# Loading the first layer's weights from a clear queue, and starting fc1 on three of four batches

## The chip, the cores and the metric

One core of a Trainium2 chip runs the kernel. The metric is the device time of one execution in microseconds; lower is better. Before the change the median of three runs is 1658.18 us (1657.36 to 1660.54).

## The reference

`x` is 64 batches of 128 rows by 512, all in float32. Two residual layers follow each other:

```
x = x + (einsum('bsd,bdh->bsh', x, W[cat_ids]) + b[cat_ids])          # layer 0
h = gelu(einsum('bnd,hd->bnh', x, fc1_w) + fc1_b)                      # 512 -> 2048
x = x + concat([einsum('bnh,sh->bns', h, fc2_w) + fc2_b,               # 2048 -> 384
                einsum('bnh,bph->bnp', h, experts_w[idx]) + experts_b[idx]])   # 2048 -> 128
```

`cat_ids` picks one of 64 matrices W of 512x512 for every batch, `idx` one of 16 expert matrices of 128x2048.

## The kernel before

The 64 batches go in 16 groups of four (GB = 4). Each float32 operand is split into a high part, rounded to fp32r by ScalarE, and a low part, which VectorE makes as the difference; every product is three fp32r matmuls (high by high and the two mixed ones). An operand x, y or weight is turned first where the contraction wants it, as four 128x128 transposes on TensorE (line 745) or by VectorE.

**The prologue** (before the first `groups` body) does layer 0 of the first four batches. A batch has four slices of its W (`KD` = 4), 256 KB each; slice j is `l0_slice(0, j)`. SyncE loads the slices (`load_w`, lines 340 to 349), eight slots deep; four of the slots lie in `w_raw`, four in `e_blocks`. Its order is written by hand in lines 399 to 420: the table `cats`, x of batch 0, a wait for `cats`, then the slices with, between them, one row of the bias b0 for each batch, the next batch's x, the table `exps`, fc1's bias `b1`, a wait for `exps` and four reads of that table; then the experts' weights. ScalarE casts a slice (`w_high`), VectorE subtracts (`w_low`), TensorE multiplies (line 784) and adds the bias row by a matmul of one row (line 782). `y_sum` adds x to the result on VectorE, `turn_y` transposes it on TensorE, `y_high` and `y_low` split it into `y_t`.

fc1 and fc2's own weights come through `load_prep(t)` on ScalarE's queue, are transposed by `turn_prep(t)` and split by `prep_high(t)` and `prep_low(t)`: tiles 0 to 4 beside the prologue, from tile 5 on two in each step of the first group. From tile 5 on, `turn_prep(t)` waits until `prep_low(t - 1)` is done, since all use the bank `ps_t`.

**The groups' loop** has 16 chunks c of 128 hidden columns. TensorE's `fc1(g, c)` is 12 matmuls of 512 columns (four batches of 128 rows side by side), into `ps_e` for even and `ps_h` for odd c; ScalarE applies `gelu`, VectorE splits the result into `h`; `fc2(g, c)` is 12 matmuls of 512 columns. Two slices of the next group's layer 0 stand between them in some chunks. All queues run in the order that the program writes; semaphores hold them together. In the first chunk the program before writes, for ScalarE, `gelu(0, 0)` and then `prep_high(5)` and `prep_high(6)`; for VectorE `h_high`, `prep_low(5)`, `h_low`, the turn of the next experts, `prep_low(6)`.

## Time and profile before

| | us |
|---|---|
| median of the runs | 1658.18 |
| the profiled execution's own time | 1657.96 |
| its span | 1656.2 |
| TensorE busy | 1637.2 |
| VectorE busy | 1314.8 |
| ScalarE busy | 554.1 |
| DMA moved | 243.44 MB |

The profile is of one execution. Its span, from the first to the last instruction, lies 1.8 us under that execution's own time. TensorE is busy for 99% of the span; a busy time counts an instruction that runs at half the clock with its full length. The page's slices are 41 us long, so that the prologue, which ends near 40 us, fills the first; questions about it go to the views by time.

### The profile page before, as it was taken

The numbers are of one execution on the slowest core, as the hardware profiler recorded it, in microseconds if no ns is written. First come the engines' busy times: TensorE is split into PE (matmuls) and PEld (weight loads), VectorE is DVE, ScalarE is ACT, GpSimd is POOL, SyncE is SP. The second block draws the span as 40 slices with busy tenths as digits, with TensorE's granted clock in tenths as the row PEclk, the third lists the DMA queues.
The fourth block names the chain that finished last, engine by engine and source line by source line (L and its number), as shares of the span: only waits on it lengthen the run. The fifth ranks groups of instructions, "written<-read, shape, count | busy, mean of one in ns | idle before, by whom it ended". The sixth has DMA issues, their size and how long they took to land.

```text
span 1656.2 us, 27997 instructions
## 1 busy us (share of the span) xinstructions
PE 1637.2 (99%) x7064; PEld 1320.6 (80%) x7064; DVE 1314.8 (79%) x2004; ACT 554.1 (33%) x926; POOL 214.4 (13%) x195
## 2 busy tenths in 40 slices
PE   7999999999999999999999999999999999999999
PEld 4788887888888888888888888888888887888887
DVE  5787978788787887877878788787878878788865
ACT  4343333333333333333333333333333333333321
POOL 0110200202020120200202011020200202002100
PEclk8899999999999999999999999999999999999999
DMA  7665555546465454664546555454654546555410
GB/s 218 175 187 136 164 151 155 144 139 167 130 175 145 143 157 115 174 161 142 153 115 183 146 161 142 141 159 133 168 157 135 152 114 180 162 144 148 134 52 26
DMA packets 303178, 243.44 MB, mean 147 GB/s; under 512 B 34152, under 2 KB 234984, under 8 KB 303084
## 3 DMA queue, kind: packets, MB, share of 16 engines
q1 hardware_dynamic: 255852, 203.75, 45.1%
q10 hardware_dynamic: 47232, 38.82, 7.7%
q14 instruction: 82, 0.67, 0.1%
q8 instruction: 12, 0.20, 0.1%
HBM read 209.93 MB, written 32.51 MB: 146 GB/s over the span
## 4 chain that ended last, share of the span: by engine, by line
PE 97%; issue 1%; SPq 1%; DMA 1%; DVE 1%; ACT 0%; DVEq 0%
PE ps_out L812 42%; PE ps_e L797 21%; PE ps_h L797 21%; PE ps_y L784 10%; PE ps_t L745 1%; PE ps_h L784 0%; SPq L316 0%; DMA x_blocks<-in_x 0%; DMA e_blocks<-in_L_cond_W 0%; DMA exps<-in_itok_B 0%; SPq L348 0%; PE ps_e L745 0%; PE ps_h L782 0%; DVE w_split L602 0%; DVE y L637 0%
## 5 line engine op out<-in xcount | busy, mean ns | idle before, releaser
L812 PE MATMUL ps_out<-w2e,h 128*128 128x512 f32 x3072 | 756.6, 395 | 0.0
L812 PEld LDWEIGHTS ps_out<-w2e,h 128*128 128x128 f32 x3072 | 575.5, 188 | 137.8
L797 PE MATMUL ps_e<-y_t,w 128*128 128x512 f32 x1536 | 378.2, 396 | 0.5 <-DVE y_t L602 0.5
L797 PE MATMUL ps_h<-y_t,w 128*128 128x512 f32 x1536 | 376.4, 394 | 0.0
L797 PEld LDWEIGHTS ps_e<-y_t,w 128*128 128x128 f32 x1536 | 289.1, 189 | 68.9 <-issue 3.8
L797 PEld LDWEIGHTS ps_h<-y_t,w 128*128 128x128 f32 x1536 | 289.6, 189 | 65.3
L646 DVE STREAM_TRANSPOSE e_whole<-e_blocks 128x512 f32<-128x512 f32 x256 | 279.1, 1090 | 0.0
L528 ACT CAST w2e<-e_whole 128x512 fp32r<-128x512 f32 x256 | 158.7, 620 | 355.3 <-DVE e_whole L646 355.3
L671 DVE CAST h<-g_raw 128x512 fp32r<-128x512 f32 x256 | 125.6, 491 | 182.8 <-ACT g_raw L542 182.7
L461 POOL TENSOR_TENSOR x_raw<-x_raw,b_all 128x512 f32<-128x512 f32 x60 | 87.3, 1455 | 1286.3 <-DMA x_raw<-in_x 1238.5
L497 ACT CAST w_split<-w_raw 128x512 fp32r<-128x512 f32 x244 | 145.2, 619 | 213.3 <-DMA w_raw<-in_L_cond_W 122.5
L602 DVE TENSOR_TENSOR w2e<-e_whole,w2e 128x512 fp32r<-128x512 f32 x256 | 199.8, 780 | 18.1 <-ACT w2e L528 17.9
L602 DVE TENSOR_TENSOR w_split<-w_raw,w_split 128x512 fp32r<-128x512 f32 x244 | 164.6, 708 | 43.1 <-ACT w_split L497 42.9
L784 PE MATMUL ps_y<-w_split,x_t 128*128 128x512 f32 x732 | 190.8, 396 | 3.2 <-DVE w_split L602 2.7
L602 DVE TENSOR_TENSOR h<-g_raw,h 128x512 fp32r<-128x512 f32 x256 | 186.3, 728 | 8.4
L542 ACT ACTIVATE g_raw<-ps_e,b 128x512 f32<-128x512 f32 x128 | 88.1, 689 | 247.5 <-PE ps_e L797 241.5
L784 PEld LDWEIGHTS ps_y<-w_split,x_t 128*128 128x128 f32 x732 | 137.2, 189 | 37.4 <-issue 5.1
L542 ACT ACTIVATE g_raw<-ps_h,b 128x512 f32<-128x512 f32 x128 | 88.0, 688 | 167.3 <-PE ps_h L797 159.6
L664 DVE CAST w2e<-w2e 128x512 fp32r<-128x512 f32 x256 | 116.4, 455 | 0.0
L471 POOL TENSOR_TENSOR resid<-y,b_all 128x384 f32<-128x384 f32 x64 | 87.1, 1361 | 75.5 <-DMA out<-resid 74.5
L617 DVE STREAM_TRANSPOSE x_whole_t<-x_blocks 128x512 f32<-128x512 f32 x60 | 64.8, 1079 | 37.9 <-DMA x_blocks<-in_x 37.9
L503 ACT CAST x_t<-x_whole_t 128x512 fp32r<-128x512 f32 x60 | 37.2, 620 | 60.0 <-DVE x_whole_t L617 60.0
(68 smaller groups left out, 459.3 us busy)
## 6 DMA issues: line engine op xcount, KB each, us to landing
e_blocks<-in_L_cond_experts_w SPq DMA_DIRECT2D x1024, 64.0 KB, 2.5
w_raw<-in_L_cond_W SPq DMA_DIRECT2D x248, 256.0 KB, 4.0
out<-resid SPq DMA_DIRECT2D x64, 256.0 KB, 2.6
b_all<-in_L_cond_b SPq DMA_DIRECT2D x60, 256.0 KB, 4.2
x_raw<-in_x SPq DMA_DIRECT2D x60, 256.0 KB, 4.7
x_blocks<-in_x SPq DMA_DIRECT2D x240, 64.0 KB, 3.2
y_rows<-y ACTq DMA_DIRECT2D x60, 256.0 KB, 3.5
x_blocks<-y_rows ACTq DMA_DIRECT2D x240, 64.0 KB, 2.7
```

What stands on the lines that cost most here:

```text
L461: nc.gpsimd.tensor_tensor(x_raw[:, :], x_raw[:, :], b0_all[:, :], ALU.add).then_inc(xb_ready, 1)
L471: nc.gpsimd.tensor_tensor(resid[:, b, 0:SHARED], y[:, b, 0:SHARED], b2_all[:, :], ALU.add)
L497: nc.scalar.copy(split_slot(G, j)[:, 0, :], w_slot(G, j)).then_inc(w_hi, 1)
L528: nc.scalar.copy(experts_of(c % 2, 0), e_whole[:, :].rearrange("p (q v n) -> p q v n", q=GB // 2, v=2))\
L542: nc.scalar.activation(g_raw[:, c % 2, :], h_bank(c)[:, :], ACT.Gelu, bias=b1[:, c:c + 1])\
L602: return nc.vector.tensor_tensor(dst, whole, high.bitcast(F32), ALU.subtract)
L646: nc.vector.transpose(e_whole[:, :].rearrange("p (a q) -> p a q", q=Q), src).then_inc(e_turned, 1)
L664: nc.vector.tensor_copy(ring[:, c % 2, :, :, 1, :], w2[:, :, c, SHARED - P:].unsqueeze(2).to_broadcast([P, 2, GB // 2, P]))\
L671: nc.vector.tensor_copy(h[:, c % 2, 0, :], g_raw[:, c % 2, :]).then_inc(h_hi, 1)
L784: last = nc.tensor.matmul(l0_bank(G, b)[:, :], x_halves(G, b)[:, a, k, :], split_slot(G, j)[:, w, :], start=(k == 0 and n == 0), stop=(k = ...
L797: last = nc.tensor.matmul(h_bank(c)[:, :], w1[:, w, k, c * P:(c + 1) * P], y_t[:, a, k, :, :].rearrange("p b s -> p (b s)"), start=(k == 0 ...
L812: last = nc.tensor.matmul(ps_out[b][:, :], h[:, c % 2, a, b * S:(b + 1) * S], fc2_columns(c, c % 2, w, b), start=(c == 0 and n == 0), stop ...
```

## The change

1. SyncE's head: `exps` is issued right behind `cats`, and is waited for only after the last slice of W. x of batch 0 and `b1` go to ScalarE's queue. The slices of batch 0 are loaded singly, those of batches 1 to 3 in pairs of 512 KB (`FIRST_W`, `load_first_w`); a pair waits until both of its slots are free. The bias row and the next batch's x follow a batch's last slice.
2. ScalarE's queue: x of batch 0, `load_prep(0)` and `b1`, then `load_prep(1)` behind the first `w_high`, `load_prep(2)` behind the second, `load_prep(3)` behind the fifth.
3. fc1 of chunks 0 and 1 is done in two parts. The matmuls on batches 0 to 2 (384 columns) are written around the last `turn_y`: half of chunk 0's before it, the rest and chunk 1's behind it. The matmuls on batch 3 (128 columns) stand where fc1 stood.
4. In the first chunk `prep_high(5)` stands before `gelu`, and `prep_low(5)` before `h_high`. (This moves the first prep tile in chunk 0 of every group, but only the first group has such tiles.)

```diff
--- before.py
+++ after.py
@@ -47,6 +47,7 @@
     S0SLOTS = 5
     AHEAD = 3
     L0_STEPS = (2, 3, 5, 7, 9, 10, 11, 12)
+    FIRST_W = ((0,), (1,), (2,), (3,), (4, 5), (6, 7), (8, 9), (10, 11), (12, 13), (14, 15))
     PSLOTS = 3
     Q = 32
     NPREP = NC + NS * NQ
@@ -113,7 +114,7 @@
         cats_in = sem("cats_in")
         exps_in = sem("exps_in")
         prep_in = [sem(f"prep_in{i}") for i in range(PSLOTS)]
-        w0_in = [sem(f"w0_in{i}") for i in range(W0SLOTS)]
+        w0_in = [sem(f"w0_in{i}") for i in range(len(FIRST_W))]
         w_in = [sem(f"w_in{i}") for i in range(WSLOTS)]
         y_stored = sem("y_stored")
         y_blocks_in = sem("y_blocks_in")
@@ -337,16 +338,20 @@
                     sp.dma_start(x_blocks[i * Q:(i + 1) * Q, :].rearrange("q (j n) -> q j n", n=P), src)\
                       .then_inc(x_blocks_in, 16)
 
+            def load_first_w(n, cat):
+
+                j, m = FIRST_W[n][0], len(FIRST_W[n])
+                after(sp, w_lo, j + m - W0SLOTS)
+                k, slot = j % KD, j % W0SLOTS
+                dst = w_raw[:, slot:slot + m, :] if slot < WSLOTS + 2 else e_blocks[:, 1, slot - WSLOTS - 2:slot - WSLOTS - 2 + m, :]
+                src = l0_w[bass.ds(cat, 1), :, :].rearrange("o (p k) n -> (o p) (k n)", k=KD)[:, k * D:(k + m) * D]
+                sp.dma_start(dst.rearrange("p k n -> p (k n)"), src).then_inc(w0_in[n], 16)
+
             def load_w(G, j, cat):
 
-                if first(G):
-                    after(sp, w_lo, j - W0SLOTS + 1)
-                else:
-                    after(sp, w_lo, G * NC + j - WSLOTS + 1)
-                k = j % KD
-                src = l0_w[bass.ds(cat, 1), :, :].rearrange("o (p k) n -> k (o p) n", k=KD)[k]
-                sp.dma_start(w_slot(G, j), src)\
-                  .then_inc(w0_in[j % W0SLOTS] if first(G) else w_in[j % WSLOTS], 16)
+                after(sp, w_lo, G * NC + j - WSLOTS + 1)
+                src = l0_w[bass.ds(cat, 1), :, :].rearrange("o (p k) n -> k (o p) n", k=KD)[j % KD]
+                sp.dma_start(w_slot(G, j), src).then_inc(w_in[j % WSLOTS], 16)
 
             def load_b0(G, b, cat):
                 after(sp, xb_ready, (G - 1) * GB + b)
@@ -397,25 +402,19 @@
                       .then_inc(out_stored, 16)
 
             sp.dma_start(cats[:, :], cat_ids.rearrange("(o n) -> o n", o=1)).then_inc(cats_in, 16)
-            load_first_x(0)
+            sp.dma_start(exps[:, :], exp_ids.rearrange("(o n) -> o n", o=1)).then_inc(exps_in, 16)
             sp.wait_ge(cats_in, 16)
-            first_experts = []
-            for j in range(NC):
-                if j % KD == 0:
-                    cat = category(0, j // KD)
-                load_w(0, j, cat)
-                if j % KD == 0:
-                    sp.dma_start(b0_rows[:, j // KD, :], l0_b[bass.ds(cat, 1), :]).then_inc(b0_rows_in[j // KD], 16)
-                if j % KD == KD - 2 and j // KD + 1 < GB:
-                    load_first_x(j // KD + 1)
-                if j == 1:
-                    sp.dma_start(exps[:, :], exp_ids.rearrange("(o n) -> o n", o=1)).then_inc(exps_in, 16)
-                    sp.dma_start(b1[:, :].rearrange("p (u c) -> p u c", c=QUAD), fc1_b.rearrange("(u p c) -> p u c", p=P, c=QUAD))\
-                      .then_inc(b1_in, 16)
-                if j == 2:
-                    sp.wait_ge(exps_in, 16)
-                if 2 <= j < 2 + GB:
-                    first_experts.append(index(exps, j - 2, exp_w.shape[0]))
+            for n, slices in enumerate(FIRST_W):
+                b = slices[0] // KD
+                if slices[0] % KD == 0:
+                    cat = category(0, b)
+                load_first_w(n, cat)
+                if slices[-1] % KD == KD - 1:
+                    sp.dma_start(b0_rows[:, b, :], l0_b[bass.ds(cat, 1), :]).then_inc(b0_rows_in[b], 16)
+                    if b + 1 < GB:
+                        load_first_x(b + 1)
+            sp.wait_ge(exps_in, 16)
+            first_experts = [index(exps, b, exp_w.shape[0]) for b in range(GB)]
             load_experts(0, 0, first_experts, range(GB))
             load_experts(0, 1, first_experts, [0])
 
@@ -490,7 +489,7 @@
         def _(act):
             def w_high(G, j):
                 if first(G):
-                    act.wait_ge(w0_in[j % W0SLOTS], 16 * (j // W0SLOTS + 1))
+                    act.wait_ge(w0_in[[j in slices for slices in FIRST_W].index(True)], 16)
                 else:
                     after(act, w_in[j % WSLOTS], 16 * ((G - 1) * (NC // WSLOTS) + j // WSLOTS + 1))
                 after(act, l0_done, j - S0SLOTS + 1 if first(G) else G * NC + j - 1)
@@ -533,8 +532,9 @@
                     return
                 act.wait_ge(prep_turned, t + 1)
                 nc.scalar.copy(prep_dst(t, 0), four(prep_bank(t))).then_inc(prep_hi, 1)
-                for u in prep_later(t):
-                    load_prep(act, u)
+                if t > 0:
+                    for u in prep_later(t):
+                        load_prep(act, u)
 
             def gelu(g, c):
                 after(act, fc1_done, g * NC + c + 1)
@@ -542,8 +542,10 @@
                 nc.scalar.activation(g_raw[:, c % 2, :], h_bank(c)[:, :], ACT.Gelu, bias=b1[:, c:c + 1])\
                     .then_inc(gelu_done, 1)
 
-            for t in range(PSLOTS):
-                load_prep(act, t)
+            act.dma_start(resid[:, 0, :], x[0, :, :]).then_inc(first_x_in[0], 16)
+            load_prep(act, 0)
+            act.dma_start(b1[:, :].rearrange("p (u c) -> p u c", c=QUAD), fc1_b.rearrange("(u p c) -> p u c", p=P, c=QUAD))\
+               .then_inc(b1_in, 16)
 
             act.wait_ge(ident_ready, 1)
             nc.scalar.activation(g_raw[:, 0, 0:1], ident[:, 0:1], ACT.Gelu)
@@ -551,10 +553,14 @@
             x_high(0, 0)
             for j in range(AHEAD):
                 w_high(0, j)
+                if j + 1 < PSLOTS:
+                    load_prep(act, j + 1)
             for j in range(NC):
 
                 if j + AHEAD < NC:
                     w_high(0, j + AHEAD)
+                if j == 1:
+                    load_prep(act, PSLOTS)
                 if j % KD == 1 and j > KD:
                     y_high(0, j // KD - 1)
                 if j % KD == KD - 2 and j // KD + 1 < GB:
@@ -578,8 +584,10 @@
                             store_y(g + 1, b)
                         for b in summed_in(c - 2):
                             load_y_blocks(g + 1, b)
+                    if c == 0:
+                        prep_high(prep_in_step(g, c, 0))
                     gelu(g, c)
-                    for n in range(PREP_RATE):
+                    for n in range(1 if c == 0 else 0, PREP_RATE):
                         prep_high(prep_in_step(g, c, n))
                 if more:
                     for b in range(GB):
@@ -715,8 +723,11 @@
                     if c == 0 and not first(g):
                         for b in range(GB):
                             result(g - 1, b)
+                    if c == 0:
+                        prep_low(prep_in_step(g, c, 0))
                     h_high(g, c)
-                    prep_low(prep_in_step(g, c, 0))
+                    if c > 0:
+                        prep_low(prep_in_step(g, c, 0))
                     h_low(g, c)
                     turn_next_e(g, c, more)
                     prep_low(prep_in_step(g, c, 1))
@@ -785,6 +796,23 @@
                                             start=(k == 0 and n == 0), stop=(k == KD - 1 and n == 2))
                 last.then_inc(l0_done, 1)
 
+            def fc1_part(c, at, end, tiles):
+
+                for k in tiles:
+                    for n, (a, w) in enumerate(((0, 0), (1, 0), (0, 1))):
+                        last = nc.tensor.matmul(h_bank(c)[:, at * S:end * S], w1[:, w, k, c * P:(c + 1) * P],
+                                                y_t[:, a, k, at:end, :].rearrange("p b s -> p (b s)"),
+                                                start=(k == 0 and n == 0), stop=(k == KD - 1 and n == 2))
+                return last
+
+            def fc1_ahead(c, tiles):
+
+                pe.wait_ge(y_lo, GB - 1)
+                if c == 1:
+                    pe.wait_ge(y_ready, GB)
+                pe.wait_ge(prep_lo, prep_count("fc1", c))
+                fc1_part(c, 0, GB - 1, tiles)
+
             def fc1(g, c):
                 if c == 0:
                     after(pe, y_lo, (g + 1) * GB)
@@ -792,12 +820,7 @@
                     pe.wait_ge(prep_lo, prep_count("fc1", c))
 
                 after(pe, gelu_done, g * NC + c - 1)
-                for k in range(KD):
-                    for n, (a, w) in enumerate(((0, 0), (1, 0), (0, 1))):
-                        last = nc.tensor.matmul(h_bank(c)[:, :], w1[:, w, k, c * P:(c + 1) * P],
-                                                y_t[:, a, k, :, :].rearrange("p b s -> p (b s)"),
-                                                start=(k == 0 and n == 0), stop=(k == KD - 1 and n == 2))
-                last.then_inc(fc1_done, 1)
+                fc1_part(c, GB - 1 if first(g) and c < 2 else 0, GB, range(KD)).then_inc(fc1_done, 1)
 
             def fc2(g, c):
                 after(pe, h_lo, g * NC + c + 1)
@@ -825,7 +848,10 @@
                     turn_x(j // KD + 1)
                 if j % KD == 0 and j > 0:
                     turn_y(j // KD - 1)
+            fc1_ahead(0, range(KD // 2))
             turn_y(GB - 1)
+            fc1_ahead(0, range(KD // 2, KD))
+            fc1_ahead(1, range(KD))
 
             def body(g, more):
                 for c in range(NC):
```

SyncE's queue from its first issue. Before (`resid` is x of a batch here, `y` the bias row):

```order
L399 DMA cats<-in_itok_B_0_63 1x64
L325 DMA resid<-in_x 128x512
L316 TENSOR_LOAD cats [waits cats_in]
L316 ISA x2
L348 ISA
L348 DMA w_raw<-in_L0_cond_W 128x512
L408 ISA
L408 DMA y<-in_L0_cond_b 1x512
L348 ISA
L348 DMA w_raw<-in_L0_cond_W 128x512
L412 DMA exps<-in_itok_B_0_15 1x64
L413 DMA b1<-in_L1_cond_fc1_b 128x4x4
```

Now:

```order
L404 DMA cats<-in_itok_B_0_63 1x64
L405 DMA exps<-in_itok_B_0_15 1x64
L317 TENSOR_LOAD cats [waits cats_in]
L317 ISA x2
L348 ISA
L348 DMA w_raw<-in_L0_cond_W 128x512
L348 ISA
L348 DMA w_raw<-in_L0_cond_W 128x512
L348 ISA
L348 DMA w_raw<-in_L0_cond_W 128x512
L348 ISA
L348 DMA w_raw<-in_L0_cond_W 128x512
```

The read of `cats` is followed by four slices; the reads and the wait for `exps` are gone from between them.

TensorE's queue from the last matmuls of the prologue's layer 0 to fc1 of chunk 1. Before:

```order
L784 MATMUL ps_h<-w_split,h 128x512 x3
L745 MATMUL ps_y<-ident,y 128x128 [waits y_lo,y_ready]
L745 MATMUL ps_y<-ident,y 128x128 x3
L745 MATMUL ps_t<-ident,prep_raw 128x128 [waits x_lo,prep_lo,prep_in1]
L745 MATMUL ps_t<-ident,prep_raw 128x128 x3
L797 MATMUL ps_e<-y_t,w1 128x512 [waits prep_lo,y_lo]
L797 MATMUL ps_e<-y_t,w1 128x512 x11
L745 MATMUL ps_t<-ident,prep_raw 128x128 [waits x_lo,prep_lo,prep_in0]
L745 MATMUL ps_t<-ident,prep_raw 128x128 x3
L797 MATMUL ps_h<-y_t,w1 128x512 [waits prep_lo]
L797 MATMUL ps_h<-y_t,w1 128x512 x11
```

Now:

```order
L795 MATMUL ps_h<-w_split,h 128x512 x3
L803 MATMUL ps_e<-y_t,w1 128x384 [waits prep_lo,y_lo]
L803 MATMUL ps_e<-y_t,w1 128x384 x5
L756 MATMUL ps_y<-ident,y 128x128 [waits y_lo,y_ready]
L756 MATMUL ps_y<-ident,y 128x128 x3
L803 MATMUL ps_e<-y_t,w1 128x384 [waits prep_lo,y_lo]
L803 MATMUL ps_e<-y_t,w1 128x384 x5
L803 MATMUL ps_h<-y_t,w1 128x384 [waits prep_lo,y_ready,y_lo]
L803 MATMUL ps_h<-y_t,w1 128x384 x11
L756 MATMUL ps_t<-ident,prep_raw 128x128 [waits x_lo,prep_lo,prep_in1]
L756 MATMUL ps_t<-ident,prep_raw 128x128 x3
L803 MATMUL ps_e<-y_t,w1 128x128 [waits prep_lo,y_lo]
```

24 matmuls of 384 columns have come before the first tile of the loop (`ps_t`), and 12 of 128 columns follow that tile; 12 more follow the next one.

VectorE's queue in the first chunk, from the low part of the experts to the turn of the next ones. Before:

```order
L602 TENSOR_TENSOR w2e<-e_whole,w2e 128x2x2x128 [waits e_hi]
L671 CAST h<-g_raw 128x512 [waits gelu_done]
L602 TENSOR_TENSOR w1<-ps_t,w1 128x4x128 [waits prep_hi]
L602 TENSOR_TENSOR h<-g_raw,h 128x512 [waits h_hi]
L646 STREAM_TRANSPOSE e_whole<-e_blocks 128x512 [waits e_lo]
L602 TENSOR_TENSOR w1<-ps_t,w1 128x4x128 [waits prep_hi]
```

Now:

```order
L610 TENSOR_TENSOR w2e<-e_whole,w2e 128x2x2x128 [waits e_hi]
L610 TENSOR_TENSOR w1<-ps_t,w1 128x4x128 [waits prep_hi]
L679 CAST h<-g_raw 128x512 [waits gelu_done]
L610 TENSOR_TENSOR h<-g_raw,h 128x512 [waits h_hi]
L654 STREAM_TRANSPOSE e_whole<-e_blocks 128x512 [waits e_lo]
L610 TENSOR_TENSOR w1<-ps_t,w1 128x4x128 [waits prep_hi]
```

The difference for tile 5 (`w1<-ps_t`) has moved before the cast that waits for gelu.

## Rows read from the trace of the kernel before

**Rows 1.** The page: TensorE's granted clock in 40 slices of the span.
```profile
PEclk8899999999999999999999999999999999999999
```

**Rows 2.** Waits of TensorE from 60 us to the end, the longest.
```profile
PE ps_t L745 <- issue: 1.4, 1, 1.4
```

**Rows 3.** The chain of waits, up to 40 us: start us, us, what.
```profile
4.32 3.47 DMA exps<-in_itok_B
...
23.33 0.85 PE ps_t L745 x4
...
27.61 0.47 PE ps_out L745 x4
28.09 0.70 PE ps_y L784 x3
...
31.60 1.05 PE ps_y L782 x2
32.65 0.91 PE ps_y L784 x3
...
38.46 0.70 DVE y L637
```

**Rows 4.** Timeline of SyncE, its first loads of W.
```profile
2.92 0.35 SPq L348 DMA_DIRECT2D w_raw<-in_L_cond_W  x1
...
8.69 0.34 SPq L348 DMA_DIRECT2D w_raw<-in_L_cond_W  x1
```

**Rows 5.** Timeline of TensorE: start us, us, instruction, xcount [idle before <-releaser].
```profile
8.98 2.90 PE L784 MATMUL ps_y<-w_split,x_t 128*128 128x512 f32 x6 [2.73 <-DVE w_split L602]
...
12.81 0.64 PE L745 MATMUL ps_out<-ident,prep_raw 128*128 128x128 f32 x4
...
18.27 1.05 PE L784 MATMUL ps_h<-w2e,h 128*128 128x512 f32 x3 [1.98 <-DVE h L602]
```

**Rows 6.** Stretches of 2 us: busy us of each engine, PEclk, DMA share, GB/s.
```profile
4.00:6.00 2.00, 1.70 (x8) 1.58 (x8) 0.00 (x0) 0.56 (x1) 0.00 (x0) 1.00 1.01 369
...
8.00:10.00 2.00, 1.01 (x3) 0.86 (x4) 1.33 (x2) 0.73 (x2) 0.00 (x0) 1.00 0.89 195
...
38.00:40.00 2.00, 1.22 (x6) 0.80 (x5) 0.69 (x1) 0.00 (x0) 0.00 (x0) 0.87 0.44 147
```

**Rows 7.** The chain of waits, 39 to 60 us.
```profile
39.20 1.04 PE ps_y L745 x4
...
40.27 0.59 ACT y_t L508
...
41.63 5.17 PE ps_e L797 x12
46.80 2.02 issue
...
49.55 4.35 PE ps_h L797 x12
...
54.37 2.80 PE ps_out L812 x12
...
57.64 2.77 PE ps_e L797 x12
```

**Rows 8.** The DMA view of 0 to 60 us: KB each, median us to landing.
```profile
prep_raw<-in_L_cond_fc_w ACTq DMA_DIRECT2D x10, 256.0 KB, 3.8
```

**Rows 9.** The DMA view of 7 to 8 us: packets.
```profile
DMA packets 478, 0.26 MB, mean 255 GB/s; under 512 B 356, under 2 KB 356, under 8 KB 478
```

**Rows 10.** Timelines of VectorE and ScalarE in the first chunk.
```profile
48.64 0.68 DVE L602 TENSOR_TENSOR h<-g_raw,h 128x512 fp32r<-128x512 f32 x1
49.24 1.12 DVE L646 STREAM_TRANSPOSE e_whole<-e_blocks 128x512 f32<-128x512 f32 x1
...
46.84 0.69 ACT L542 ACTIVATE g_raw<-ps_e,b 128x512 f32<-128x512 f32 x1 [3.55 <-PE ps_e L797]
```

**Rows 11.** Timeline of SyncE, the experts' first loads.
```profile
22.06 14.79 SPq L383 DMA_DIRECT2D e_blocks<-in_L_cond_experts_w  x20
```

## The prediction

> **What bounds the kernel now.** First the clock row of the page [rows 1]: TensorE is at full speed from the third slice on; anything to win from it lies in the first 80 us. Then its waits behind 60 us [rows 2]: one stop of 1.4 us and almost nothing else in 1600. From there it works without a break, so whatever time the start gives up should come off the end, one for one. Then the chain of waits of the start [rows 3, 7], which has two stages.
>
> Stage A is layer 0 of the first group, up to 38.4 us, where the last slice ends and VectorE takes the sum [rows 3]. SyncE issues the first slice at 2.92 and the fourth only at 8.69 [rows 4], because it stood 3.47 us behind `exps` [rows 3]. TensorE runs two slices at 8.98 and then waits; the first prep tile after them starts at 12.81, and the next stop is 1.98 us before 18.27 [rows 5]. Transfers are tight too: 369 GB/s at a DMA share of 1.01 between 4 and 6 us [rows 6]. From 27.6 on nothing is missing, and layer 0's last part takes 38.4 - 27.6 = 10.8 us.
>
> Stage B reaches from 38.4 to fc2's start at 54.37: 15.9 us [rows 7]. Its work at full clock is four transpose groups of 0.47 us [rows 3] (the last `turn_y` and tiles 5, 6 and 7) and two fc1 chunks of 2.77 us [rows 7], 7.4 us. The other 8.5 are idle time and half clock. Idle are 0.8 us behind the last sum, 0.5 us before fc1, and the 2.02 us before tile 6, in which TensorE waits for `prep_low(5)`, itself behind gelu. The clock falls to half (1.2 of 2.4 GHz) in 38 to 40 us [rows 6], so that fc1 takes 5.17 and then 4.35 us instead of 2.77 [rows 7]. Half clock is also seen as 0.85 us for a transpose group that takes 0.47 later, at 23.33 [rows 3], and as 2.90 us for six matmuls at 8.98 [rows 5], where three take 0.70 at full clock.
>
> **Stage A, changed.** The first slice still hangs on `cats`: 2.9 us. The next three follow at about 0.45 us each (an issue is 0.35 us [rows 4], plus an address step), the fourth near 4.7. The first pair goes out near 6.2, the second near 6.8, where before the fifth slice was behind the fourth at 8.69. The `exps` wait and its four reads cost nothing now; they lie behind the last slice and delay only the experts (below). x of batch 0 is ScalarE's first transfer and `load_prep(0)` its second; the tile should start TensorE at 4.3 as before, give or take 0.3. The first matmul moves from 8.98 to about 8.4, since the slice is there when ScalarE is free.
>
> What moves the other way is prep tile 1: issued at the head before, now behind the first cast, near 7 us. It takes 3.8 us to land [rows 8], up to 4.7 in a full queue, so it is there near 11.5, and TensorE's queue has it ahead of slice 2. So the stretch that began at 12.81 [rows 5] begins near 11.6. Tile 2, x of batch 2 and the pairs are wanted later than they land: with all 3.9 MB that are ahead of x of batch 2 at about 300 GB/s (between the 195 and 369 of [rows 6]) it lands near 16, and is wanted at 17.4.
>
> From 11.6 on, TensorE's work up to tile 3, at full clock [rows 3], is: tile 1 0.47, slice 2 0.70, bias row and slice 3 1.96 (1.05 + 0.91), slice 4 0.70, a wait of 0.2 for the sum, `turn_y` and tile 2 0.94, slice 5 0.70, x of batch 2 0.47, slice 6 0.70, bias row and slice 7 1.96: together 8.8, so tile 3 starts at 20.4 where it started at 27.61. Adding 10.8 gives 31.2. The clock rises only after some continuous work; how far into this stretch it is at half I can bound by 0 and by 1.6 us (the 4.35 - 2.77 of a short half-clock stretch [rows 7]), and take the middle, 0.8. Layer 0 ends at 32.0 instead of 38.4: **6.4 us gained**, bounds 4 (each pair some 2.5 us late) and 7.2.
>
> `b1` is 512 pieces of 16 bytes and now lies ahead of the first slice. Where it ran before, 356 small packets shared a microsecond with 0.26 MB, at 255 GB/s [rows 9] beside 369: a third lost for one microsecond, so some 0.4 us for all 512. ScalarE's earlier work hides it, as the first slice has a microsecond to spare. The Trainium skill (DMA: Bandwidth & Descriptors, Specifications) speaks against the move: below 512 B a transfer is a read-modify-write and misses line rate. That agrees with the row; if its price were a whole microsecond on the first slice, my estimate by it is a sum 0.5 us higher.
>
> **Stage B, changed**, counted from layer 0's end (T). A 384-column matmul is bounded by the 128-column transpose, 0.118 us (0.47/4) [rows 3], and 512 columns, 0.231 us (2.77/12) [rows 7]; linear between them it is about 0.18. Six take 1.1 us and cover the last sum (0.70 [rows 3]); `turn_y` ends at 1.6, 18 more at 4.8, covering the 0.59 [rows 7] and 0.6 us of the last y's split; tile 5 ends at 5.3. A 128-column matmul is bounded by 0.118 (the transpose of the same shape) and 0.231 (no cheaper than 512); I take the lower, since shape and weight load are alike. Twelve: 1.4 us, to 6.7. `prep_high(5)` and `prep_low(5)` (0.6 each) end at 6.5: the 2.02 us wait is gone. Tile 6 to 7.2, twelve more to 8.6.
>
> What is late next is tile 7: it waits for `prep_low(6)`, which on VectorE now stands behind gelu (6.7 to 7.4, 0.69 [rows 10]), `h_high` to 7.9, `h_low` 0.6, the turn of the experts 1.1, itself 0.6 (start to start, and 1.12 [rows 10]): 10.2. Its data, issued near 5.3, lands at 9.1 to 9.7. So TensorE waits 1.6 us there, and fc2 starts at T + 10.7 instead of T + 15.9: 5.2 less. By work the same comes out: 7.4, plus 24 x (0.18 + 0.12 - 0.23) = 1.6, plus 1.6 idle. Such a gap has cost the clock before: 0.8 us idle before 39.2 and the fall in 38 to 40 us [rows 6, 7], 2.0 us before 48.8 and a chunk of 4.35. I charge it once, 1.6. **3.6 us gained**, bounds 5.2 (clock stays) and 2.5. With 128 columns at 0.231, tile 6 ends 1.4 later, gelu too, and fc2 starts near T + 12.0, but nearly without the gap and the clock's fall: 3.9 gained, so this unknown hardly moves the sum.
>
> The experts' first loads are 20 issues in 14.79 us [rows 11]. They start near 20 rather than 22.06, since the reads of `exps` now lie before them, and the 16 for the first quad end near 32, landed at 34.5. VectorE wants them at T + 2.9 = 34.9; a miss of up to 2 us there is hidden by fc1. Later chunks find the engines in the same relation to fc2's start as before, so the rest stays.
>
> Sum: 6.4 + 3.6 = 10.0 us off 1657.96, the profiled execution, gives **1648.0 us**. That execution lies 0.2 under the median of 1658.18, which is nothing beside the bounds.
>
> **Rivals.** About 0.2%, 3.3 us, is what a measurement of this kernel can tell from no change.
>
> *The transfers bound stage A.* The pairs come as wholes of 512 KB, and prep tiles 1 to 3 move into the time when slices 2 to 7 fly. For: a share of 1.01 at 369 GB/s in 4 to 6 us [rows 6]. Against: at 8 to 10 us only 195 GB/s moved, in part because nothing more was asked for. Then stage A gives 2 to 4 us, the whole 1651 to 1654.
>
> *Both stages at their best*: no half clock after the gap, none in stage A: 1645.
>
> *The start's gain is lost later.* VectorE or the POOL queue is late in the first group, as at the 1.4 us stop [rows 2], and stops grow by what was won; within 0.2% if 7 us of 10 go. Against: everything in the chunks hangs on TensorE's own progress.
>
> *Slower: fp32r matmuls of under 512 columns are not single-pass.* All fp32r matmuls of the trace have 512 columns, so it does not exclude this. The float32 bias row takes 1.05 us for 512 columns [rows 3], 2.05 ns a column. At that price 384 columns take 0.79 us, 24 x (0.79 - 0.18) = 14.6 us more, 24 x (0.26 - 0.12) = 3.4 for the narrow ones, less the gap of 1.6 and the 1.6 of clock, 14.8 in all: 1663. It decides from some 0.60 us a 384-column matmul on.
>
> **Chances.** Forecast (1645.5 to 1650.5) 0.55; transfers bound stage A 0.22; both at best 0.10; lost later 0.08, most of it within 0.2%; slower by narrow matmuls 0.05. Of the second, 0.20 is still over 0.2% faster. Faster 0.86, same 0.09, slower 0.05. The range 1643.5 to 1653.5 holds the first three but for their edges.
>
> **What would show it.** SyncE's fourth slice near 4.7 us; tile 1 starting near 11.6; layer 0's last matmul near 32; no stop before tile 6 and one of 1 to 2 us before tile 7; fc2's first matmul near 42.7 instead of 54.4; TensorE's waits behind 60 us still under 2.5 us. Wrong would be: fc1's 384-column matmuls over 0.25 us at full clock, stops for slices between 12 and 30 us, or new stops in the first group.

## The result, and the profile after

| | median us | runs | span of the profiled execution |
|---|---|---|---|
| before | 1658.09 | 1657.36 to 1660.54 | 1656.2 |
| the change | 1675.62 | 1671.99 to 1678.38 | 1674.7 |

The change makes the kernel slower: the ratio is 1.0115, with a 95% interval of 1.0097 to 1.0134. The forecast was 1648.0 us. The page of the changed kernel first, against [rows 1] and the table of times before:

```profile
PE 1636.9 (98%) x7088; PEld 1320.3 (79%) x7088; DVE 1319.1 (79%) x2004; ACT 556.1 (33%) x926; POOL 217.6 (13%) x195
...
PEclk9999999999999999999999999999999999999999
...
q14 instruction: 95, 0.78, 0.2%
...
PE 77%; issue 8%; SPq 7%; DMA 4%; DVE 3%; ACT 1%; DVEq 0%
...
L795 PE MATMUL ps_y<-w_split,x_t 128*128 128x512 f32 x732 | 191.9, 397 | 24.3 <-DVE x_t L610 22.2
```

TensorE's busy time is what it was (1636.9 against 1637.2 us), though the start is at full clock from 11.4 us on, and the span is 18.5 us longer. The chain, which was TensorE for 97% before, is now TensorE for 77%, and layer 0's matmuls of the next group (L795) stand idle for 24.3 us, 22.2 of them for VectorE's `x_t`. The row `q14 instruction` is the one to remember: 95 fetches of instructions. The page of before has 82:

```profile
q14 instruction: 82, 0.67, 0.1%
```

The start went much as forecast. TensorE's timeline of the changed kernel (start us, us, instruction):

```profile
8.53 2.90 PE L795 MATMUL ps_y<-w_split,x_t 128*128 128x512 f32 x6 [2.09 <-DVE w_split L610]
11.23 0.69 PE L756 MATMUL ps_t<-ident,resid 128*128 128x128 f32 x4
13.54 0.75 PE L756 MATMUL ps_out<-ident,prep_raw 128*128 128x128 f32 x4 [1.61 <-DMA prep_raw<-in_L_cond_fc_w]
14.04 0.94 PE L795 MATMUL ps_y<-w2e,x_t 128*128 128x512 f32 x3
14.91 1.12 PE L793 MATMUL ps_y<-y,g_raw 1*128 1x512 f32 x2
...
33.00 0.97 PE L795 MATMUL ps_h<-w_split,h 128*128 128x512 f32 x3
33.81 1.21 PE L803 MATMUL ps_e<-y_t,w 128*128 128x384 f32 x6
...
36.40 2.25 PE L803 MATMUL ps_h<-y_t,w 128*128 128x384 f32 x12
38.48 0.63 PE L756 MATMUL ps_t<-ident,prep_raw 128*128 128x128 f32 x4
38.87 1.53 PE L803 MATMUL ps_e<-y_t,w 128*128 128x128 f32 x12
40.57 0.72 PE L756 MATMUL ps_t<-ident,prep_raw 128*128 128x128 f32 x4 [0.16 <-issue]
41.05 1.54 PE L803 MATMUL ps_h<-y_t,w 128*128 128x128 f32 x12
43.99 0.72 PE L756 MATMUL ps_t<-ident,prep_raw 128*128 128x128 f32 x4 [1.41 <-DMA prep_raw<-in_L_cond_fc_w]
44.47 3.05 PE L835 MATMUL ps_out<-w2e,h 128*128 128x512 f32 x12
```

Layer 0 ends at 34.0 us (38.4 before, [rows 3]) and fc2 starts at 44.5 (54.1 before, by the timeline; the chain of [rows 7] has it at 54.37). 384 columns cost 2.08/12 = 0.17 us a matmul, 128 columns (40.57 - 38.87 less the wait of 0.16)/12 = 0.13. The stop before tile 6 is gone, and there is one of 1.41 us before tile 7.

The waits of TensorE for `x_t` from 60 us to the end (us in total, times, longest), in the changed kernel and then in the kernel before, where they come beside the one stop of [rows 2]:

```profile
PE ps_y L795 <- DVE x_t L610: 22.2, 13, 2.8
```

```profile
PE ps_y L784 <- DVE x_t L602: 0.3, 1, 0.3
```

Thirteen stops for `x_t`, one in each pass of the loop of groups: 1.7 us each. TensorE's branches back lie 102.4 us apart on average (248.1 to 1578.7 us in 13 passes) instead of 100.2 (257.3 to 1560.1). So TensorE reaches the loop's first branch 9.2 us sooner and loses 28 us in the 13 passes. The stops are 22 of these. Twice, at 984 and 1394 us, the granted clock also falls to half (1.2 GHz) for 3.4 us, behind stops of 2.5 and 2.6 us, and a chunk's twelve matmuls take 4.50 us instead of 2.91; the rest, some 3 us, is spread over the passes. The chain of waits through one of the thirteen stops (start us, us, what), followed back on SyncE's queue:

```profile
247.89 0.05 SPq L301
247.94 3.90 issue
251.84 0.06 SPq L301
...
252.28 0.16 SPq L317
252.44 1.56 issue
...
256.94 0.35 SPq L354
...
258.93 0.37 SPq L338
...
260.50 4.73 DMA x_blocks<-in_x
```

```profile
266.36 0.82 DVE w_split L610 x2
...
267.53 0.70 DVE x_t L610
...
268.35 1.65 PE ps_y L795 x6
```

At 247.89 SyncE branches back to the loop's start and then stands for 3.90 us, for no semaphore ("issue"). It runs three instructions and stands again, for 1.56 us. Then come the reads of `exps`, the first slice at 256.94, the four blocks of x at 258.93; they land at 265.2, VectorE turns them, ScalarE and VectorE split them, and TensorE starts at 268.35, 2.8 us late. In the kernel before the same place shows the first stall alone. (That one varies: 2.5 to 4.0 us over the passes of both kernels, 3.1 and 3.2 on average, so it is not what changed.) Its instructions of the loop's line and its reads of the tables there (count, durations in ns, first and last start us):

```profile
L300 PEldq COMPARE_BRANCH  x1: 243/243/243, 257.3 to 257.3; - x1
...
L300 SPq COMPARE_BRANCH  x1: 53/53/53, 257.8 to 257.8; - x1
...
L300 SPq FUSED_REGOPS  x1: 64/64/64, 260.7 to 260.7; - x1
```

```profile
L316 SPq TENSOR_LOAD <-exps x4: 263/266/278, 260.8 to 262.8; - x4
L316 SPq TENSOR_LOAD <-cats x1: 275/275/275, 263.5 to 263.5; - x1
```

From the branch at 257.8 to 260.7 it stands 2.9 us, and the five reads follow each other up to 263.5 without a hole. SyncE issues the first slice at 264.3, 6.9 us behind TensorE's own branch at 257.3; in the changed kernel it is 8.8 us (256.94 - 248.1). Over all passes it is 5.6 to 7.0 us before and 7.4 to 8.8 now.

### The profile page after: what moved, and what is told of

Read it like the earlier page. It is cut to its first block, busy times and chain, and to the rows that moved or that the text cites. A ratio compares the mean times of both kernels' runs of the same rounds, so it can differ in the third digit from the quotient of the medians.

```text
span 1674.7 us, 28030 instructions
## 1 busy us (share of the span) xinstructions
PE 1636.9 (98%) x7088; PEld 1320.3 (79%) x7088; DVE 1319.1 (79%) x2004; ACT 556.1 (33%) x926; POOL 217.6 (13%) x195
## 3 DMA queue, kind: packets, MB, share of 16 engines
q1 hardware_dynamic: 254316, 203.48, 44.5%
## 4 chain that ended last, share of the span: by engine, by line
PE 77%; issue 8%; SPq 7%; DMA 4%; DVE 3%; ACT 1%; DVEq 0%
PE ps_out L835 32%; PE ps_h L803 17%; PE ps_e L803 17%; PE ps_y L795 10%; DMA x_blocks<-in_x 3%; SPq L317 2%; SPq L395 1%; SPq L388 1%; SPq L338 1%; DVE e_whole L654 1%; PE ps_t L756 1%; DVE w_split L610 1%; SPq L354 1%; DVE x_t L610 1%; ACT g_raw L542 1%
## 5 line engine op out<-in xcount | busy, mean ns | idle before, releaser
L803 PE MATMUL ps_h<-y_t,w 128*128 128x512 f32 (+1 forms) x1548 | 378.8, 394 | 0.0
L803 PE MATMUL ps_e<-y_t,w 128*128 128x512 f32 (+1 forms) x1548 | 377.1, 393 | 0.0
L795 PE MATMUL ps_y<-w_split,x_t 128*128 128x512 f32 x732 | 191.9, 397 | 24.3 <-DVE x_t L610 22.2
L610 DVE TENSOR_TENSOR w_split<-w_raw,w_split 128x512 fp32r<-128x512 f32 x244 | 168.3, 723 | 34.5 <-ACT w_split L496 34.0
L795 PEld LDWEIGHTS ps_y<-w_split,x_t 128*128 128x128 f32 x732 | 136.5, 189 | 61.9 <-DVE w_split L610 27.8
L502 ACT CAST x_t<-x_whole_t 128x512 fp32r<-128x512 f32 x60 | 37.3, 621 | 73.1 <-DVE x_whole_t L625 73.1
```

Source lines behind the costliest of these rows:

```text
L610: return nc.vector.tensor_tensor(dst, whole, high.bitcast(F32), ALU.subtract)
L795: last = nc.tensor.matmul(l0_bank(G, b)[:, :], x_halves(G, b)[:, a, k, :], split_slot(G, j)[:, w, :], start=(k == 0 and n == 0), stop=(k = ...
L803: last = nc.tensor.matmul(h_bank(c)[:, at * S:end * S], w1[:, w, k, c * P:(c + 1) * P], y_t[:, a, k, at:end, :].rearrange("p b s -> p (b s)"),
```

## Why: the first theory and its rival

The change takes 20 instructions from SyncE's queue ahead of the loop: six slices that need no issue of their own at three instructions each (two set the address), x of batch 0 and `b1`. The trace counts 885 SyncE instructions to the first branch back in the kernel before and 865 in the changed one; a pass is 406 in both. **Theory F**: instructions come in blocks. 0.78 MB / 95 is 8.2 KB a fetch, and SyncE's fetches inside a pass lie 121 to 139 of its instructions apart. The loop's start has moved to three instructions before the end of a block. Every pass jumps there, waits for the block, and needs the next one at once. 95 - 82 = 13 more fetches fit 13 passes. The times of the fetches in the trace say the same. In every pass of the changed kernel a fetch starts 0.9 to 2.4 us behind the branch, and SyncE goes on 1.5 to 2.3 us after that start. A second starts 0.6 to 0.8 us later, when the three instructions are done, and SyncE goes on 1.5 to 1.7 us after that. A third follows by the eighth instruction. In the kernel before the first two fetches come in the same way, but SyncE does not stand for the second, and the third comes only at the 116th instruction or behind it. The Trainium skill (Runtime: NRT & Kernel Launch, Instruction fetch mechanics) says that a taken branch whose target is not in the engine's small instruction memory forces a fetch before execution goes on. The 2.5 to 4.0 us behind every branch of SyncE agree with it. The Trainium skill gives blocks of 16 KiB there; SyncE's here are 8 KB. Why the first fetch starts only 0.9 to 2.4 us behind the branch no run shows.

**Rival P** is near the forecast's own worry: TensorE, ten microseconds ahead after the start, finds the next group's x late, and stays ahead.

In the experiments the loop is moved by unused reads of `exps`, three instructions each, in the first group where SyncE waits anyway. They change no output.

### after_pad21: the loop back in its place

```diff
                         load_expert_bias(0, first_experts)
+                        for _ in range(7):
+                            index(exps, 0, exp_w.shape[0])
```

> The changed kernel with 7 unused reads of the table exps more on SyncE's queue, in chunk 1 of the first group, where SyncE waits anyway: 21 more instructions ahead of the loop, so that the loop begins one instruction from where it began in the kernel before. Theory F (instruction fetch: the loop's start on SyncE has moved to three instructions ahead of a block's end, so each pass fetches a second block at once, 1.5 us late): 1646 to 1649 us, no stop of 1.5 us behind the third instruction of a pass, five 8 KB fetches a pass instead of six, and TensorE's waits for x_t under 1 us in all. Rival P (TensorE is 10 us ahead of SyncE after the start and so finds the transfers of the next x late in each group): 1672 to 1679, as without the reads.

Measured: 1654.01 us (1653.01 to 1658.98), ratio to before 0.9985 (0.9970 to 0.9999); 22 us less than the change measures without the seven useless reads (1.3% by the ratios to the kernel before, each taken beside it). The waits of TensorE and the page's row of fetches:

```profile
PE ps_y L797 <- DVE x_t L612: 1.4, 2, 0.9
```

```profile
q14 instruction: 82, 0.67, 0.1%
```

22.2 us of stops became 1.4, 95 fetches 82. This speaks against P, but not by itself: in this execution TensorE comes to the loop's first branch at 250.8 us, 2.7 later than in the change. pad21_prep1 below decides it: there TensorE is at the branch at 247.5 us, ahead of the change's 248.1, and its stops for `x_t` are 1.6 us in all. P falls. But 1654 is not the 1646 to 1649 that was expected; that is the matter of the second half.

### after_pad3: the smallest move

The same with `range(1)`.

> The same with one read, 3 instructions: the loop begins exactly at a block's start, if the stall is where the trace shows it. Theory F: 1646 to 1649 us, the same as with 21. Rival P: 1672 to 1679. If a wider distance from the block's end matters (the fetch is late for other reasons), between the two.

Measured: 1654.40 us (1651.39 to 1659.84), ratio 0.9985 (0.9970 to 1.0000), 82 fetches, and no second stall: one read, three instructions, is enough for that. The time misses the expected range like the run before. TensorE still stops for `x_t` four times, 3.7 us in all against 1.4 in after_pad21, with the first slice issued 5.9 to 7.6 us behind its branch, 0.3 us later on average; why is open. The three instructions that stood alone at a block's end now stand at a start.

### before_pad108: the fault put into the kernel before

```diff
+                    if first(g) and 5 <= c < 14:
+                        for _ in range(4):
+                            index(exps, 0, exp_w.shape[0])
                     if more and c == NC - 1:
                         load_expert_bias(g + 1, next_idx)
```

> The kernel before with 36 unused reads of exps, four in each of chunks 5 to 13 of the first group: 108 instructions, which with the 20 that the change removed make 128, one block of 8 KB; so its loop begins where the changed kernel's does. Theory F: 1680 to 1688 us (1658 and the 22 to 29 us that the changed kernel loses in the loop), with a stop of 1.5 us behind the third instruction of each pass. Rival P: 1658 to 1662, since its start is as late as before.

Measured: 1681.84 us (1676.78 to 1683.68), ratio 1.0152 (1.0126 to 1.0177). Its waits, its fetches, and the two stalls in one pass by the chain:

```profile
PE ps_y L787 <- DVE x_t L605: 18.2, 13, 2.7
```

```profile
q14 instruction: 96, 0.79, 0.2%
```

```profile
254.23 3.17 issue
...
257.99 1.45 issue
```

The original kernel, with nothing of the change in it, loses 25 us when its loop starts at this place, by the same thirteen stops (the profiled execution is the fastest of the four, 1676.78 us, and loses 20). Its TensorE is at the first branch at 254.0 us, later than in the change, which speaks against P once more. F is shown from both sides, and 108 + 20 = 128 instructions fit as the length of a block.

### after_pad123: half the distance

The same loop of reads in chunks 5 to 13, 41 in all, in the changed kernel.

> The changed kernel with 41 unused reads of exps, 123 instructions, in chunks 5 to 13 of the first group: the block's end should then lie eight instructions behind the loop's first instead of three. SyncE needs some 1.4 us to get there instead of 0.6, and a block takes some 2.1 us after the one before it. Theory F: the second stall shrinks from 1.5 to 0.7 us and moves to behind the eighth instruction; TensorE's waits for x_t fall to about half, the whole 1660 to 1667 us. If the loss came with any second fetch, whatever its place: 1672 or more; if only the exact place counts: 1653 to 1656.

Measured: 1669.31 us (1666.55 to 1673.00), ratio 1.0078 (1.0050 to 1.0106), 96 fetches. The stall:

```profile
256.15 0.83 issue
```

It is there behind the eighth instruction of each pass, and lasts 0.75 to 1.01 us, 0.83 on average. The size and place are those of F. The stops for `x_t` are 14.1 us in 11 passes instead of 22.2 in 13, and the time is 2 us above the range that I gave: the stops fall less than the stall. The second block takes about 2.1 us after the first (0.6 + 1.5, and 1.35 + 0.75); by my estimate from these a loop that starts some 14 instructions or more before a block's end should be safe, which was not run.

### reads_late: the stall kept, the need for it moved

```diff
-                idx = first_experts if first(g) else [index(exps, g * GB + b, exp_w.shape[0]) for b in range(GB)]
+                idx = first_experts
                 for c in range(NC):
                     if more:
                         load_l0_in(g + 1, c)
+                    if c == 0 and not first(g):
+                        idx = [index(exps, g * GB + b, exp_w.shape[0]) for b in range(GB)]
```

> The changed kernel, no padding; in SyncE's loop the four reads of exps at the head of a pass move behind the first loads (slices 0 and 1, bias, x and its four blocks), which takes 2.6 us of SyncE's time from before the loads that TensorE waits for. The number of instructions and the place of the loop stay, so the double fetch of 1.5 us should still be seen. Theory F with its place in the chain: the stall stays but is covered; 1652 to 1656 us, TensorE's waits for x_t under 2 us. If what costs the time is not SyncE's lateness at the head of a pass but something else that moves with the padding: still 1670 or more.

Measured: 1659.44 us (1655.99 to 1662.17), ratio 1.0013 (0.9999 to 1.0027): 95 fetches as in the change, the second stall still there in each pass (1.4 to 1.8 us), and yet 16 us faster. So it is SyncE's lateness at the head of a pass that costs. Not all of it is covered: the waits for `x_t` have given way to others, for the slices that SyncE now issues later by the four reads:

```profile
PE ps_y L797 <- DVE w_split L612: 4.8, 9, 0.9
```

The median lies above the expected range. SyncE's first loads, issued 7.4 to 8.8 us behind TensorE's branch in the change, come at 5.0 to 6.6 here and 5.6 to 7.5 in after_pad21.

## The second question: what the change is worth without the fault

### before_fc1 and before_fc1_again: fc1's two parts alone

Parts 3 and 4 of the change in the kernel before; SyncE's queue as it was.

> The kernel before with only fc1's first two chunks in two parts and the first prep tile of chunk 0 ahead of gelu (parts 3 and 4 of the change); SyncE's queue is untouched, TensorE's is longer by as many instructions as in the change. Theory F: 1651 to 1654 us (5.2 us off the stage behind layer 0, less what a lower clock there costs), and no stops in the loop. Theory that the moved code on TensorE or VectorE makes the loop slow: 1672 or more. Rival P: between, from 1655 on, since TensorE is ahead by half as much.

Measured: 1654.26 us (1652.51 to 1656.88), ratio 0.9982 (0.9971 to 0.9993), with 2.9 us of stops in all behind 60 us, 1.4 of them for `x_t`. TensorE's longer queue does no harm to the loop. Measured again beside two others:

> fc1's two parts alone, as measured at 1654.3: the theory that the new heads gain 1.3 us in layer 0 says 1 to 1.5 us over the padded change; if they gain nothing there, the same as it within the interval.

1653.48 us (1650.95 to 1654.72), ratio 0.9983 (0.9974 to 0.9992), against 1652.88 for the padded change (after_pad21_again, below): 0.6 us apart, within the intervals.

### sync_only_pad21: the new heads alone

Parts 1 and 2 with the seven reads.

> The change without fc1's parts (SyncE's and ScalarE's new heads alone), with the 7 reads that put the loop back in its place. Theory A (the new heads are worth what the prediction said, and the padded kernel is held up elsewhere): 1651 to 1653 us. Theory B (the new heads gain next to nothing, since layer 0 of the first group ends by when the clock rises, and the trace of before was one in which it fell late): 1655 to 1658 us.

Measured: 1657.96 us (1654.28 to 1663.71), ratio 1.0014 (1.0000 to 1.0028). Theory B: on the median the new heads gain nothing. The profiled execution is the fastest of the ten, 1654.28 us. Its timeline at the start of stage B:

```profile
34.45 0.91 PE L753 MATMUL ps_y<-ident,y 128*128 128x128 f32 x4 [0.78 <-DVE y L645]
...
36.77 5.29 PE L805 MATMUL ps_e<-y_t,w 128*128 128x512 f32 x12 [0.55 <-DVE y_t L610]
44.09 0.72 PE L753 MATMUL ps_t<-ident,prep_raw 128*128 128x128 f32 x4 [2.03 <-issue]
44.56 4.59 PE L805 MATMUL ps_h<-y_t,w 128*128 128x512 f32 x12
```

Stage B is the old one, line by line as in [rows 7]: 0.78, 0.55 and 2.03 us idle and both chunks at half clock.

All profiled executions together show what stage A is worth:

| start as | kernel | layer 0 ends | fc2 starts |
|---|---|---|---|
| before | before | 38.4 | 54.1 |
| | before_pad108 | 35.3 | 50.8 |
| | before_fc1, again | 36.2, 37.0 | 47.4, 48.2 |
| new heads | sync_only_pad21 | 33.7 | 49.4 |
| | the change | 34.0 | 44.5 |
| | after_pad21, again | 37.0, 36.8 | 47.5, 47.5 |
| | after_pad3, reads_late, after_pad123 | 37.3, 36.1, 37.7 | 47.9, 46.6, 48.2 |
| new heads, tile 1 early | late_prep1, pad21_prep1 | 33.3, 32.8 | 43.8, 43.2 |

Layer 0 with the old head ends at 36.7 on average, with the new at 36.1, and each spreads over 3 to 4 us, so that this difference is not clear of the spread. The spread goes with the granted clock: the five executions in which TensorE was not at full clock for 11.4 to 14.4 us of the time before layer 0's end have it at 32.8 to 35.3, the eight with 16.4 to 21.8 us at 36.1 to 38.4. Among the five the new heads end 1.3 to 1.6 us sooner than the old one (33.7 and 34.0 against 35.3). after_pad21's own timeline, against the change's above:

```profile
11.32 1.06 PE L758 MATMUL ps_t<-ident,resid 128*128 128x128 f32 x4
13.99 1.13 PE L758 MATMUL ps_out<-ident,prep_raw 128*128 128x128 f32 x4 [1.61 <-DMA prep_raw<-in_L_cond_fc_w]
14.77 1.63 PE L797 MATMUL ps_y<-w2e,x_t 128*128 128x512 f32 x3
16.33 2.07 PE L795 MATMUL ps_y<-y,g_raw 1*128 1x512 f32 x2
18.33 1.65 PE L797 MATMUL ps_y<-w2e,x_t 128*128 128x512 f32 x3
```

Three matmuls of slice 2 take 1.63 us here and 0.94 there, and the bias row 2.07 instead of 1.12: TensorE was still at 1.2 GHz, up to 21.6 us in this execution, with the same start and the same stop of 1.61 us for tile 1, where the change's trace was at 2.4 from 11.4 on. The trace of before was itself unlucky: at half clock from 19.0 to 25.8 us, where before_pad108, whose start is the same code, was at full clock, and ended layer 0 3.1 us earlier.

Stage B is steady: 15.7, 15.6 and 15.7 us in the three traces with the old fc1, 10.5 to 10.8 with the change, 11.2 in both of before_fc1.

### late_prep1 and pad21_prep1: tile 1 at the head again

```diff
             load_prep(act, 0)
+            load_prep(act, 1)
             act.dma_start(b1[:, :].rearrange("p (u c) -> p u c", c=QUAD), fc1_b.rearrange("(u p c) -> p u c", p=P, c=QUAD))\
                .then_inc(b1_in, 16)
...
-                if j + 1 < PSLOTS:
+                if 1 < j + 1 < PSLOTS:
                     load_prep(act, j + 1)
```

In reads_late first:

> reads_late with prep tile 1 issued at the head of ScalarE's queue again, behind tile 0, ahead of b1. TensorE's wait of 1.6 us for that tile, before slice 2, should go, against slices 0 to 3 that share the queue with 256 KB more. If the wait is what holds the start up: 1 to 2 us under reads_late. If the slices are then later by as much, or the clock rises at the same time anyway: no difference that can be measured.

Measured: 1657.62 us (1653.52 to 1659.44), ratio 1.0003 (0.9989 to 1.0017): 1.8 us under reads_late by the medians, with intervals that overlap. Then in after_pad21, compared with it on one chip:

> The changed kernel with the 7 reads (the loop in its place) and prep tile 1 issued at the head of ScalarE's queue. The start should lose its wait for that tile, 1.0 to 2.2 us in the traces of the changed kernels, and nothing is lost in the loop: 1651 to 1653 us, 4 to 6 under the kernel before, and 1 to 2 under the next. If the wait is covered by when the clock rises: no different from the next.

Measured: **1649.52 us** (1648.01 to 1654.14), ratio 0.9966 (0.9957 to 0.9976), 1.5 us under the expected range, beside

> The changed kernel with the 7 reads, as measured at 1654.0, beside the others on one chip: 2.5 to 5 us under the kernel before (0.9970 to 0.9985).

1652.88 us (1650.12 to 1654.67), ratio 0.9980 (0.9971 to 0.9989). The best kernel here is 6.9 us under the kernel before, and 3.4 under the padded change. Its timeline where the others stop for tile 1:

```profile
9.17 2.90 PE L798 MATMUL ps_y<-w_split,x_t 128*128 128x512 f32 x6 [2.09 <-DVE w_split L613]
11.86 1.06 PE L759 MATMUL ps_t<-ident,resid 128*128 128x128 f32 x4
12.71 0.78 PE L759 MATMUL ps_out<-ident,prep_raw 128*128 128x128 f32 x4
13.24 0.94 PE L798 MATMUL ps_y<-w2e,x_t 128*128 128x512 f32 x3
```

The stop of 1.6 us is gone, and slice 2 already runs at full clock. The gain is above the 1.6 us of the stop in this comparison; that the rest is a clock that rises more surely when TensorE is not stopped there fits both traces of this start (full clock from 14.3 and 13.1 us), but two traces don't show it.

## Why the prediction was wrong

The step that failed is "From there it works without a break, so whatever time the start gives up should come off the end, one for one", and with it "so the rest stays". The change put the loop's time at nothing; it measured 28 us longer, against the 9.2 us by which TensorE came to its first branch sooner. In place of "the rest stays" the runs showed a second stall of 1.5 us on SyncE in each of 13 passes, because the change moved the loop's start in SyncE's instruction stream. SyncE had no slack for it: with the first slice issued 5.6 to 7.0 us behind TensorE's branch the loop had one stop of 0.3 us, with 7.4 to 8.8 it had one in every pass. Nothing in the forecast asked how long SyncE takes from its branch to its first load, or why. The first stall is in the trace of before, 2.9 us of nothing behind a branch. The second is not; that it threatened could only be worked out from the places of the fetches. The rival that was meant to end slower priced narrow matmuls; the runs give it no support (0.17 us for 384 columns). "The start's gain is lost later" had 0.08 and came nearest, but it looked for late work of VectorE or POOL in the first group and bounded the loss by the gain. A stop that comes with every pass has no such bound: 13 x 1.7.

Point by point:

- **SyncE's head.** The fourth slice near 4.7 us and no wait for `exps`: so it came, and it didn't matter.
- **Stage A, 6.4 us.** Measured: 4.4 between the two profiles, 0.6 between the averages of eleven. Two terms were mis-sized. Tile 1 came at 13.5 us, not 11.6: issued at 6.49, it took 7.0 us to land instead of 3.8 to 4.7, beside the slices. Up to 16 us the median prep tile took 6.7 us and a pair of slices 7.0 to 8.2, with 368 GB/s at a DMA share of 1.00 between 12 and 14 us. So the rival "The transfers bound stage A", with 0.22, held in part: this tile came 1.9 us late, and layer 0 ended at 34.0 instead of 32.0. And the base was one execution with 6.8 us of half clock in it, which I took as part of the kernel: the same code in before_pad108 ends 3.1 us sooner. The clock's own term, 0 to 1.6 with a middle of 0.8, was up to 3.0 (37.0 against 34.0, same code).
- **Stage B, 3.6 us with a fall of the clock, 5.2 without.** Measured 15.7 to 10.5 on the averages: 5.1. The terms for 384 and 128 columns held (0.17 and 0.13 us for 0.18 and 0.12), as did the new stop before tile 7, 1.4 for 1.6 us; it waits for the tile's own data rather than for `prep_low(6)`. In seven of the ten traces with fc1 in two parts the clock does not fall there, in three (pad21_prep1, after_pad21_again, before_fc1_again) it falls at the stop for tile 7 and stays at half for 3.4 us. The charge of 1.6 belonged to a chance of three in ten.
- **`b1`'s small pieces at the head.** The first matmul came at 8.5 us, forecast 8.4; neither the 0.4 us of my row nor the microsecond that I had put on the rule of the Trainium skill (DMA: Bandwidth & Descriptors, Specifications) is seen there. ScalarE's earlier work would hide a small delay, and no run moved `b1` alone, so its price stays open.
- **The experts' loads** were no bound.

What stays open: the two stages give 5.7 us on the average of the profiles, the medians of the padded change 3.2 and 3.5 us. The loop of after_pad21 has 1.4 us of stops that the kernel before has not (0.3); the rest, about a microsecond, is within the spread of the runs. Open too is what starts the first fetch behind a branch so late.

## What to carry to other kernels

Where an engine's queue is a rolled loop, its place in the instruction stream is part of the kernel: taking instructions away ahead of it can cost more than they did. Count the fetches on the page (the `instruction` queues) before and after every change, look at what the queue that issues the loads does behind its backward branch, and put what the next pass needs first ahead of all else there. And take the base of a sum at a start from several executions, since with the same code the clock of the first 50 us moved layer 0's end by 3 us.

## What the hardware showed

- Behind each backward branch SyncE stands 2.5 to 4.5 us in every kernel here. A block boundary three instructions behind the target adds a second stall of 1.4 to 1.8 us, eight behind one of 0.75 to 1.01; with one at the target itself or 17 and 18 ahead of it (after_pad3, before, after_pad21) there is no second stall.
- The fetch of the next block started 0.6 to 0.9 us after SyncE had gone on in the one before it, and where SyncE stood for it, it went on 1.5 to 1.7 us after that fetch's start.
- SyncE's blocks are 8 KB, 128 instructions; the trace's other instruction queue, q8, moves 0.20 MB in 12 fetches, 16 KB each.
- fp32r matmuls of 384 and 128 columns take 0.17 and 0.13 us at full clock; nothing of the float32 price of 2.05 ns a column that the slow rival needed.
- The same start was granted full clock from 11.4 us in one execution and from 21.6 in another. In the change's loop the clock was at half for 3.4 us behind two of the 13 stops for `x_t` (of 2.5 and 2.6 us), and not behind the others, one of 2.8 us among them.
